# A first attention whose steps take the turned scores ahead of the mask matmuls and the plain scores

## The reference, cut to what matters

```python
q, k, v = (heads(x @ W.T) for W in (Wq, Wk, Wv))     # 8 x 16 x 256 x 16
att = einsum('bhtd,bhsd->bhts', q, k) / sqrt(16)
att = att + triu(full((T, T), neg), k=1)             # causal mask
w = softmax(att, axis=-1)
z = einsum('bhts,bhsd->bhtd', w, v)
return z.reshape(B, T, D) @ Wo.T
```

## Time and profile before

| | |
|---|---|
| runs | 1317.68, 1317.75, 1322.83 us, median 1317.75 |
| the profiled execution's own time | 1321.02 us |
| its span | 1319.2 us |
| TensorE matmul busy | 987.9 us, 75% |
| VectorE busy | 798.6 us, 61% |
| ScalarE busy | 368.9 us, 28% |
| GpSimd busy | 374.5 us, 28% |
| step u = 0 of round 0 starts at | 50.9 us of the span |
| the last turned scores start at | 332.9 us of the span |

### The profile page before, as it was taken

The page is one execution under the profiler, slowest core; times in us unless marked ns, Lnnn a source line. Parts: engine busy times, 40 slices in busy tenths (PEclk is TensorE's granted clock), DMA queues, the critical chain, the costliest instruction groups (busy, mean ns, idle before and its releaser), DMA issues.

```text
span 1319.2 us, 18912 instructions
## 1 busy us (share of the span) xinstructions
PE 987.9 (75%) x6860; PEld 819.5 (62%) x6860; DVE 798.6 (61%) x1642; ACT 368.9 (28%) x715; POOL 374.5 (28%) x533
## 2 busy tenths in 40 slices
PE   3787778878447105787879589899899988698883
PEld 3565666666336105666667477788778877477673
DVE  3556776664488402545444457767776775578785
ACT  1222333232212102333232243223322331233230
POOL 2112222213103773222212304432443211133332
PEclk9777998886759657999899767657765776799996
DMA  9900000000001536999994212110111000000000
GB/s 343 350 29 2 1 1 1 2 2 1 0 1 36 164 113 200 307 290 291 287 287 142 75 45 88 41 31 9 40 40 28 12 1 1 0 1 17 0 17 32
DMA packets 74683, 109.77 MB, mean 83 GB/s; under 512 B 7528, under 2 KB 63208, under 8 KB 74600
## 3 DMA queue, kind: packets, MB, share of 16 engines
q1 hardware_dynamic: 62696, 73.03, 16.8%
q0 software_dynamic: 11904, 35.66, 8.9%
HBM read 62.53 MB, written 46.14 MB: 82 GB/s over the span
## 4 chain that ended last, share of the span: by engine, by line
PE 38%; DVE 28%; POOL 9%; issue 8%; SPq 6%; DMA 5%; ACT 5%; DVEq 0%; POOLq 0%; ACTq 0%
POOL xd L430 5%; PE ZO L859 4%; DMA raw<-in_experts 4%; PE ZO L743 3%; SPq L330 3%; PE S L743 2%; PE ZO L745 2%; PE ZO L744 2%; DVE attn_w L1508 2%; DVE work L1752 2%; DVE work L1214 2%; PE S L818 2%; PE S L1028 2%; SPq L331 2%; DVE st L1205 2%
## 5 line engine op out<-in xcount | busy, mean ns | idle before, releaser
L1566 DVE TENSOR_TENSOR work<-work,S 64x256 f32<-64x256 f32 x128 | 54.2, 424 | 159.9 <-ACT work L612 159.0
L743 PE MATMUL ZO<-parts 128*128 128x256 f32 x288 | 98.3, 341 | 52.6 <-POOL parts L489 18.0
L1028 PE MATMUL S<-work,raw 128*128 128x128 f32 x512 | 77.8, 298 | 41.4 <-DMA raw<-in_experts 41.2
L401 POOL TENSOR_SCALAR veps<-mv 128x2 f32<-128x2 f32 x64 | 16.3, 255 | 318.1 <-DVE mv L1209 318.1
L743 PEld LDWEIGHTS ZO<-parts 128*128 128x128 f32 x288 | 64.8, 225 | 63.5 <-POOL parts L489 21.3
L1028 PEld LDWEIGHTS S<-work,raw 128*128 128x128 f32 x512 | 66.8, 204 | 52.4 <-DMA raw<-in_experts 52.2
L410 POOL TENSOR_SCALAR_AFFINE_SELECT work<-work 128x256 f32<-128x256 f32 x128 | 49.5, 411 | 175.6 <-ACT work L518 175.6
L744 PE MATMUL ZO<-parts 128*128 128x256 f32 x288 | 91.6, 318 | 0.0
L745 PE MATMUL ZO<-parts 128*128 128x256 f32 x288 | 91.6, 318 | 0.0
L430 POOL DMA_INDIRECT xd<-attn_w,slots x64 | 67.1, 1049 | 83.0 <-DVE slots L1462 63.8
L1017 PE MATMUL S<-ident,work 128*128 128x128 f32 x256 | 44.7, 300 | 60.4 <-DMA work<-xd 60.4
(11 more groups left out here) (283 smaller groups left out, 2731.9 us busy)
## 6 DMA issues: line engine op xcount, KB each, us to landing
raw<-in_experts SPq DMA_DIRECT2D x128, 192.0 KB, 4.1
xd<-zero SPq DMA_DIRECT2D x8, 2048.0 KB, 16.9
work<-xd POOLq DMA_DIRECT2D x64, 256.0 KB, 5.2
yd<-work SPq DMA_DIRECT2D x64, 256.0 KB, 4.6
raw<-in_ffn SPq DMA_DIRECT2D x2, 1536.0 KB, 9.9
x_sb<-in_x SPq DMA_DIRECT2D x1, 2048.0 KB, 8.4
shd<-work SPq DMA_DIRECT2D x8, 256.0 KB, 2.8
attn_w<-shd POOLq DMA_DIRECT2D x8, 256.0 KB, 3.2
```

The lines of the kernel that those rows point to most:

```text
L743: pe.matmul(dst, a(0), b(0), start=start, stop=False, skip_group_check=True)
L1028: last = pe.matmul(S[2 + i % 2][:, b * P:(b + 1) * P], raw[:, i % RING, o:o + P], xT[:, i % 2, b, c, :], start=(c == 0), stop=(c == KC - 1))
L1566: last = dve.tensor_tensor(hx[64 * half:64 * half + 64, i % 2, :], sgx[64:128, i % 2, :], S[2 + i % 2][64:128, 0:256], ALU.mult)
```

## The change

Within one call of `scores` the turned part moves to the front, with its own waits (`a_nm`, `a_exp`) ahead of it, and the waits of the plain part (`a_k`, `a_mx`) move down behind it. The mask matmuls and the plain scores follow. No instruction is added or removed, and no bank is changed: the two pairs of banks for the plain scores are there before and after.

```diff
             def scores(nb, b, u):
 
-                if nb is not None:
-                    pe.wait_ge(s["a_k"], 4 * nb + (u ^ 1) // 2 + 1)
-                    if 8 * nb + u >= 2:
-                        pe.wait_ge(s["a_mx"], 8 * nb + u - 1)
-                if b is not None:
-                    if u == 0:
-                        pe.wait_ge(s["a_nm"], b + 1)
-                    pe.wait_ge(s["a_exp"], 8 * b + u)
-                if nb is not None:
-                    for r in range(2):
-                        diagonals(M[u % 2][:, r * 512:(r + 1) * 512], mask_ts)
...
+                if b is not None:
+                    if u == 0:
+                        pe.wait_ge(s["a_nm"], b + 1)
+                    pe.wait_ge(s["a_exp"], 8 * b + u)
+                    for k in range(3):
+                        for half in range(2):
+                            for r in range(2):
+                                last = turned(r, half, k)
+                    last.then_inc(s["a_st"], 1)
+                if nb is not None:
+                    pe.wait_ge(s["a_k"], 4 * nb + (u ^ 1) // 2 + 1)
+                    if 8 * nb + u >= 2:
+                        pe.wait_ge(s["a_mx"], 8 * nb + u - 1)
+                    for r in range(2):
+                        diagonals(M[u % 2][:, r * 512:(r + 1) * 512], mask_ts)
+
                 for late in (True, False):
                     if nb is not None:
                         for r in range(2):
                             last = plain(r, late)
                 if nb is not None:
                     last.then_inc(s["a_sc"], 1)
-                if b is not None:
-                    for k in range(3):
-                        for half in range(2):
-                            for r in range(2):
-                                last = turned(r, half, k)
-                    last.then_inc(s["a_st"], 1)
```

## The result

The changed kernel took 1343.11 us (median of 6 runs, 1337.66 to 1347.63), the kernel before 1323.09 (median of 6, 1317.68 to 1324.89, its three earlier runs among them). The ratio is 1.0158, with a 95% interval of 1.0124 to 1.0193: slower by 20 us. The forecast was 1319.2 and no visible change, in a range to 1329. It was wrong. The two traces come from executions of 1321.02 and 1339.55 us.

What follows compares the result with a forecast made beforehand. No engine is full, so the chain of waits through each 37.23 us round sets the pace. Terms of -1.9 + 3.3 + 0.0 = +1.4 us on the runs' median of 1317.75 gave 1319.2 us, range 1310 to 1329.

Steps and rivals of the forecast that it cites:

- The step's length: Each step of scores on TensorE: 0.84 + 0.70 plus an entry, 1.64 us against 1.17, so 0.47 us longer.
- Step 0: Start of the round: turned scores start earlier, behind L1274; gain 0.37 us in three rounds, 0.2 in four, 1.9 in all.
- Step 2: Between two projections with no wait on either side: all 0.47 us exposed, 3.3 us over seven rounds.
- Steps 1 and 3: TensorE waits for VectorE's L1248 behind them: the extra 0.47 us hides in 0.6 to 0.7 us of idle time.
- Steps 4 and 5 even: Earlier exponential of step 4 pays for the longer step 5: net 0.0, -0.7 to +1.4 us over seven rounds.
- VectorE waits for plain scores at any step but 0: Sign named beforehand: seeing VectorE held by plain scores at steps 1 to 7 would show the prediction wrong.
- the one rival about it: Less idle time ahead of step 0 keeps PEclk up in first values: 1307.7 us; 2.2 in slow rounds; chance 0.18.
- The slower rival: Steps grow by 0.9 us, not 0.47, exposing steps 1 and 3: +10.7 us, 1328.5; chance 0.20.

Runs made afterwards that it cites:

- the run with step 0 alone: New order at step 0 only, old order at steps 1 to 7, against the kernel before: 1315.26 us, ratio 0.9924.

## Why the prediction was wrong, by its own steps

**The step's length: right.** 0.84 + 0.70 for a step was worked out, and 1.53 measured, at step 2 of the changed kernel and at step 0 with fillers. The entry of 0.21 us into 32-row matmuls is in the rows again.

**Step 0: right where the clock is at 1.00.** Turned scores start 0.05 us behind L1272 in every round looked at, and the run with step 0 alone is faster. But the term took four slow and three fast step 0s from the trace of before, as if the clock stayed as it was. In the changed kernel's later rounds step 0 is slow.

**Step 2: right**, +0.47. **Steps 1 and 3: right**, hidden, with 0.27 us of idle time still there.

**Steps 4 and 5 even: wrong**, +0.42 us in each of six rounds, 2.5 us in all. The step said that nothing else came late. It missed what stands behind the maxima of step 4 on VectorE: the output norm, on which the projection of group 3 waits. Counted from where the chain enters the step, their maxima start 0.9 us later than before (1.58 for 0.64), and VectorE, which ran through without waiting there, now idles 0.93 us for them. The norm had some slack, and 0.42 of the delay came through. "VectorE waits for plain scores at any step but 0" was named as a sign of error, and it is there. With this term corrected the sum is some +4 us, still no visible change.

**The clock: the step that failed.** The sum kept the clock of the trace of before, and the one rival about it had the wrong sign. It counted the idle time taken away ahead of step 0 and not the time that step 0 then spends in 32-row matmuls, nor any other place. In its place the traces show 43 us more at half speed, part of them waiting time. With the order at +4 us, about 15 of the 19.1 us are left to the clock; in the round taken apart it is 3.4 of 3.9. Two runs show that it is the clock and not the waits: fillers that only add work take the loss away, and one execution has rounds of both lengths from the same instructions. A third, the output norm ahead of two maxima, shows how little tips it.

The slower rival named a time, 1328.5, and a place, steps 1 and 3 exposed. Neither held. In the faster one a round that is slow throughout would win 5.11 - 2.78 = 2.3 us, not 2.2; nothing hangs on it.

**What stays open** is why the new order tips rounds into the long form. Three sets of steps (4 and 5; 1 to 3; all) make all later rounds long. All steps but 4 and 5 make only some of them long, and step 0 alone none. What the first three share is steps that are 0.47 us longer, with masks between the two sets of scores; but the fourth has them too. The kernel with masks, turned, plain at every step fits this: it has another order too, its steps keep their length, and it loses nothing. But it also starts step 0 no earlier, and no run made the steps longer in the old order, so that their length is the cause is not shown. The losses don't add up either: 8 us for steps 4 and 5, 13 for steps 1 to 3, a gain of 6 for step 0, and 20 for all eight. Each kernel has one trace, and its executions differ by up to 22 us (1309.79 to 1331.74 for the changed kernel with fillers), so how often a kernel's rounds are long is not known from the traces.

The Trainium skill (TensorE: Matmul & The Clock Gate, Why this matters for your kernels) advises against long idle gaps of TensorE between bursts of matmuls, since they bring the clock down. The traces bear it out only in part. In the changed kernel TensorE idles 1.5 us ahead of step 0 and PEclk is 0.50 behind it, and with 1.2 us of fillers in the gap it is 1.00. But the kernel before idles 2.27 us there and has 1.00 around step 0. So the length of this gap alone does not tell which kernel keeps its clock.

## What to carry to other kernels

A sum made from durations holds the clock fixed. Where a loop's rounds show both levels of the clock, price what one more stretch at half speed costs (here some 0.5 to 1.7 us each) with both signs, before any gain of a few tenths is believed. Fillers in a known gap are a cheap test of it: ten useless matmuls gave back what the reordering had lost, and eighteen made the old order 0.4% faster. Look at the whole round afterwards, since the low stretch can turn up in another place.

When a producer moves later within a step, follow its consumer's list one item further. The maxima of step 4 could wait; the norm queued behind them could not.

Keep matmuls that use the whole array out from between two sets that use different strips of it.

## What the runs showed of the hardware that was not expected

TensorE overlaps matmuls of 32 rows in different strips across program order. With four plain ones behind twelve turned ones, their loads began after the first six to eight (170.81 and 170.92, the turned ones from 170.52 to 171.27), and the step stayed as short as with the plain ones first. With the two masks between the two sets and not ahead of both, the same eighteen matmuls took 0.47 us more (1.53 for 1.06).

Useless work can shorten a program: ten filler matmuls, about 1.2 us at half clock in each of seven rounds, and the whole ran 2% faster than without them.
